# Turning row maxima in 32x32 blocks on VectorE instead of through TensorE and PSUM, and moving them on in 128-byte pieces

## The reference

```
x = x + 0.5 * ffn(layernorm(x))          # ffn: x + msa(ln(x)), then x + moe(ln(x)), top-1 of 8 experts
x = x + attn(layernorm(x))               # 16 query heads, 4 key/value heads, rotary embedding
x = x + 0.5 * ffn(layernorm(x))
scores = q @ k.T / sqrt(8);  attn = softmax(scores, axis=-1);  y = attn @ v
```

## Time and profile before

| | |
|---|---|
| time, median of 3 runs | 1510.23 us (1509.4 to 1512.35) |
| the profiled execution | 1509.52 us; its span 1507.8 us |
| TensorE busy | 1377.5 us (91%) |
| VectorE busy | 1176.0 us (78%) |
| ScalarE busy | 1102.9 us (73%) |
| granted TensorE clock, mean | 0.977 |
| DMA packets | 101485, of them 29792 under 512 B |

### The profile page before, as it was taken

How to read it: one execution, slowest core, us unless ns; L and a number is a source line. 1 busy time by engine, 2 the same in 40 slices (tenths; PEclk the granted TensorE clock), 3 DMA queues, 4 the chain that set the end, 5 groups by cost and what they waited for, 6 DMA issues and landing times.

```text
span 1507.8 us, 34954 instructions
## 1 busy us (share of the span) xinstructions
PE 1377.5 (91%) x12036; PEld 670.6 (44%) x12036; DVE 1176.0 (78%) x1898; ACT 1102.9 (73%) x2124; POOL 646.7 (43%) x983
## 2 busy tenths in 40 slices
PE   3899999999999997999999999999999999999995
PEld 1333333433338883333333333333333344335995
DVE  6888889888855348888888888888888888894541
ACT  2488877787785563888888888787878777777553
POOL 5224245542226683544364353323334543313753
PEclk8799999999999997999999999999999999999998
DMA  3644433433102425432333243333333333211234
GB/s 90 164 137 117 111 102 98 114 93 86 45 25 60 119 75 160 114 83 69 97 97 83 71 110 86 100 91 79 89 93 84 81 88 100 63 37 37 75 106 120
DMA packets 101485, 137.57 MB, mean 91 GB/s; under 512 B 29792, under 2 KB 72160, under 8 KB 101312
## 3 DMA queue, kind: packets, MB, share of 16 engines
q1 hardware_dynamic: 70768, 85.69, 19.9%
q0 software_dynamic: 24256, 45.31, 12.3%
q10 hardware_dynamic: 6288, 4.34, 1.0%
HBM read 79.05 MB, written 53.51 MB: 88 GB/s over the span
## 4 chain that ended last, share of the span: by engine, by line
PE 58%; DVE 28%; issue 7%; DMA 3%; POOL 2%; ACT 1%; SPq 0%; DVEq 0%; POOLq 0%; ACTq 0%
DVE maxima L1251 25%; PE banks L884 16%; PE banks L871 12%; PE banks L855 11%; PE banks L1610 4%; PE banks L912 4%; PE banks L1619 4%; PE banks L894 2%; PE banks L938 2%; PE banks L919 1%; DMA by_token<-work 1%; PE banks L954 1%; DVE split L1259 1%; DVE stats L1329 1%; DMA work<-sorted_x 1%
## 5 line engine op out<-in xcount | busy, mean ns | idle before, releaser
L1251 DVE TENSOR_REDUCE maxima<-banks 128x2 f32<-128x1024 f32 x768 | 924.1, 1222 | 154.9 <-PE banks L855 146.8
L1222 ACT ACTIVATE work<-banks 128x512 f32<-128x512 f32 x1536 | 829.6, 598 | 155.5 <-PE banks L871 140.6
L855 PE MATMUL banks<-K,Q 64*128 64x512 f32 x1536 | 568.2, 459 | 46.5 <-DVE maxima L1251 36.4
L871 PE MATMUL banks<-Q,K 64*128 64x512 f32 x1536 | 566.2, 450 | 0.5
L884 PE MATMUL banks<-work,V 128*18 128x256 f32 x6144 | 481.6, 386 | 1.5 <-ACT work L1222 0.8
L855 PEld LDWEIGHTS banks<-K,Q 64*128 64x128 f32 x1536 | 228.2, 189 | 200.8 <-DVE maxima L1251 135.4
L871 PEld LDWEIGHTS banks<-Q,K 64*128 64x128 f32 x1536 | 228.9, 185 | 177.4 <-ACT work L1222 128.3
L884 PEld LDWEIGHTS banks<-work,V 128*18 128x18 f32 x6144 | 103.3, 96 | 275.1 <-issue 199.8
L723 POOL TENSOR_TENSOR lo<-full,hi 128x512 fp32r<-128x512 f32 x40 | 51.1, 1278 | 245.6 <-ACT hi L1097 144.1
L1619 PE MATMUL banks<-w,work 128*128 x736 | 99.6, 279 | 0.6 <-ACT work L1653 0.6
L1673 DVE COPY work<-w 128x512 f32 x88 | 43.9, 499 | 71.8 <-PE banks L1610 58.6
(11 more groups left out here) (193 smaller groups left out, 1268.4 us busy)
## 6 DMA issues: line engine op xcount, KB each, us to landing
Q<-q_scratch SPq DMA_DIRECT2D x188, 128.0 KB, 2.6
K<-k_scratch SPq DMA_DIRECT2D x376, 64.0 KB, 2.5
Q<-zero_rows SPq DMA_DIRECT2D x182, 64.0 KB, 2.2
q_scratch<-hi POOLq DMA_DIRECT2D x40, 256.0 KB, 4.7
q_scratch<-lo POOLq DMA_DIRECT2D x40, 256.0 KB, 6.8
k_scratch<-hi POOLq DMA_DIRECT2D x20, 256.0 KB, 4.5
k_scratch<-lo POOLq DMA_DIRECT2D x20, 256.0 KB, 6.3
work<-sorted_x SPq DMA_DIRECT2D x76, 66.0 KB, 2.0
```

Source lines behind the costliest of these rows:

```text
L855: fill(nc.tensor.matmul(bank, q4[parts(j), n % SLOTS, j // 2, qt * P:(qt + 1) * P], k4[parts(j), n % SLOTS, j // 2, :], start=True, stop=T ...
L871: nc.tensor.matmul(scp[x % EXPS][:, :], k4[parts(j), n % SLOTS, j // 2, kt * P:(kt + 1) * P], q4[parts(j), n % SLOTS, j // 2, :], start=Tr ...
L1222: nc.scalar.activation(prob[:, kt, j ^ 1, :], scp[x % EXPS][:, :], ACT.Exp, scale=SCALE).then_inc(s.probs, 1)
L1251: nc.vector.tensor_reduce(c.maxima[:, at:at + 9:8], c.banks[:, k * S:(k + 2) * S].rearrange("p (m n) -> p m n", m=2), AX.X, ALU.max).then_ ...
```

## The change

The diff, cut to its core:

```diff
 class Plan:
     def group(self, n, kt):
         names = []
-        if kt == 0 and 1 <= n + 1 < self.last:
-            names += [("rows", n + 1)]
 ...
             def rows_of_max(n):
                 g = n % SLOTS
-                if n:
-                    released(sp, "rows", n)
-                else:
-                    sp.wait_ge(s.first, 2)
+                sp.wait_ge(s.max_turned, n + 1)
                 for tile in range(2):
                     r = TILE * tile + ROWS
-                    sp.dma_start(c.Q[r:r + 2, g * KSLOT:(g + 1) * KSLOT].bitcast(F32).rearrange("i (a n) -> i a n", n=P),
-                                 c.maxT[16 * tile:16 * tile + 16, n % 2 * P:(n % 2 + 1) * P].bitcast(F32))\
-                        .then_inc(s.max_rows[g], 16)
+                    dst = c.Q[r:r + 2, g * KSLOT:(g + 1) * KSLOT].bitcast(F32).rearrange("i (a b q) -> i a b q", b=4, q=32)
+                    for b in range(4):
+                        at = 32 * b + 16 * tile
+                        sp.dma_start(dst[:, :, b, :], c.maxT[at:at + 16, 32 * (n % 2):32 * (n % 2) + 32])                            .then_inc(s.max_rows[g], 16)
 ...
-            def turn_max(n):
-
-                pe.wait_ge(s.split, n + 1)
-                bank = bank_for("rows", n) if n else outp
-                ins = nc.tensor.transpose(bank[0:32, 0:P], c.split[:, 32 * (n % 2):32 * (n % 2) + 32].bitcast(F32), c.ident[:, :])
 ...
                 nc.vector.tensor_tensor(parts[:, :, 1, :], whole, parts[:, :, 0, :].bitcast(F32), ALU.subtract)\
                     .then_inc(s.split, 1)
-
-            def copy_rows(n):
                 if n >= 2:
-                    dve.wait_ge(s.max_rows[(n - 2) % SLOTS], 32 * ((n - 2) // SLOTS + 1))
-                if n:
-                    bank = ring[turns["rows", n].first % RING]
-                    filled(dve, "rows", n)
-                else:
-                    bank = outp
-                    dve.wait_ge(s.first, 1)
-                ins = nc.vector.tensor_copy(cols(c.maxT, n % 2 * P, P), bank[0:32, 0:P])
+                    dve.wait_ge(s.max_rows[(n - 2) % SLOTS], 128 * ((n - 2) // SLOTS + 1))
+                dve.wait_ge(s.split, n + 1)
+                nc.vector.transpose(cols(c.maxT, 32 * (n % 2), 32), cols(c.split, 32 * (n % 2), 32).bitcast(F32))\
+                    .then_inc(s.max_turned, 1)
 ...
-        c.maxT = sb("maxT", [32, 2 * P], F32R)
+        c.maxT = sb("maxT", [P, 2 * 32])
```

More of the change, by code:

```diff
@@ L277 @@
 Turn = namedtuple("Turn", "first end engine done")
-CONSUMER = {"max": "dve", "rows": "dve", "out": "dve", "gate": "dve", "z": "act", "q": "act", "qs": "act", "k": "act",
+CONSUMER = {"max": "dve", "out": "dve", "gate": "dve", "z": "act", "q": "act", "qs": "act", "k": "act",
             "ks": "act", "v": "act", "a": "act", "proj": "act", "n": "act", "rank": "act"}
@@ L396, in stream @@
     if True:
-        s = sems(ctx, nc, f"s{label}", "filled freed evacuated first max_hi split recip max_rows:5 q_loaded:5 k_loaded:5 "
+        s = sems(ctx, nc, f"s{label}", "filled freed evacuated max_hi split max_turned recip max_rows:5 q_loaded:5 k_loaded:5 "
                  "scores probs pv out_copied links dve_links first_stored:2 var_ready std_ready normed renormed stats:2 moments:2 added combined roped hi lo:2 "
@@ L654, in main @@
                 for g in range(SLOTS):
-                    sp.wait_ge(s.max_rows[g], 32 * len(range(g, last, SLOTS)))
+                    sp.wait_ge(s.max_rows[g], 128 * len(range(g, last, SLOTS)))
                 if label == 0:
@@ L856, in max_score @@
                                       k4[parts(j), n % SLOTS, j // 2, :], start=True, stop=True), "max", n, qt, j)
-            def turn_max(n):
-                pe.wait_ge(s.split, n + 1)
-                bank = bank_for("rows", n) if n else outp
-                ins = nc.tensor.transpose(bank[0:32, 0:P], c.split[:, 32 * (n % 2):32 * (n % 2) + 32].bitcast(F32), c.ident[:, :])
-                if n:
-                    fill(ins, "rows", n)
-                else:
-                    ins.then_inc(s.first, 1)
             def score(n, kt, j):
@@ L975, in group @@
                 for kind, i in plan.groups.get((n, kt), ()):
-                    if kind == "rows":
-                        turn_max(i)
-                    elif kind == "rank":
+                    if kind == "rank":
                         rank(i)
@@ L1262, in split_max @@
                     .then_inc(s.split, 1)
-            def copy_rows(n):
                 if n >= 2:
-                    dve.wait_ge(s.max_rows[(n - 2) % SLOTS], 32 * ((n - 2) // SLOTS + 1))
-                if n:
-                    bank = ring[turns["rows", n].first % RING]
-                    filled(dve, "rows", n)
-                else:
-                    bank = outp
-                    dve.wait_ge(s.first, 1)
-                ins = nc.vector.tensor_copy(cols(c.maxT, n % 2 * P, P), bank[0:32, 0:P])
-                if n:
-                    freed(ins, "rows", n)
-                else:
-                    ins.then_inc(s.first, 1)
+                    dve.wait_ge(s.max_rows[(n - 2) % SLOTS], 128 * ((n - 2) // SLOTS + 1))
+                dve.wait_ge(s.split, n + 1)
+                nc.vector.transpose(cols(c.maxT, 32 * (n % 2), 32), cols(c.split, 32 * (n % 2), 32).bitcast(F32))\
+                    .then_inc(s.max_turned, 1)
             def normalise(n):
@@ L1309, in group @@
                 for kind, i in plan.groups.get((n, kt), ()):
-                    if kind == "rows":
-                        copy_rows(i)
-                    elif kind == "out":
+                    if kind == "out":
                         normalise(i)
```

4 lines of the change are left out of this document (1 added, 3 removed).

## The result

The changed kernel takes 1541.8 us (median of 4 runs, 1538.02 to 1544.34) against 1511.29 us (median of 4, 1509.4 to 1513.11): ratio 1.02, 95% interval 1.0172 to 1.0228. It is slower, as forecast, but by 30.5 us where I forecast 10.8, and outside my range. The profiled execution took 1543.42 us with a span of 1541.7, against 1509.52 and 1507.8.

What follows compares the result with a forecast made beforehand. The loop between TensorE and VectorE at group ends was taken as the bound. 14.0 + 3.9 - 8.3 - 0.5 - 1.2 + 2.9 = +10.8 us gave 1521 us, forecast's own range 1512 to 1533, 0.8 range 1501 to 1534.

Steps and rivals of the forecast that it cites:

- Where the loop lies: At group ends: scores, last reduction, split, two reductions, scores; VectorE work put between split and these reductions lengthens the loop.
- The price of the turn: Block turn on VectorE behind the split: delays the next group's first reduction by 0.27 us, ends 0.22 and 0.40.
- y: Time from the block turn's start to the next reduction's start on VectorE: taken as 0.14 us, between 0.09 and 0.27.
- a: Added delay of the reduction behind the block turn: 0.13 us plus the turn's hold on VectorE, 0.27 us in all.
- First kind: 52 group ends where "rows" has "z", "a" or "n" with it: 0.27 us slower each, +14.0 us (11.4 to 20.8).
- Second kind: 26 group ends whose other filling is one long matmul: 0.15 us slower each after 0.12 us spare, +3.9 us.
- Third kind: 14 mid-stream group ends with "rows" alone: a round trip saved, 0.59 us sooner each, -8.3 us (-9.0 to -6.4).
- Starts of the streams: Group 0 of each stream: -1.2 us at the first from sooner reductions, +2.9 us at the second from late maxima.
- my 6.8 us: Landing of the last of eight transfers after the turn: 7 x 0.616 us of issuing plus 2.5 us to landing.
- Mid-stream transfers at nothing: Eight transfers per group within a stream: hidden with 1.5 us to spare in the shortest group, costed at nothing.
- the rows come late: Rival, chance 0.08: at 1.2 us an issue the last transfer is 2.6 us late in shortest groups, about 1560 us.
- -0.5 us that I had for groups 30 and 62: Groups 30 and 62, with no quarter-1 scores left: only TensorE's turn of 0.27 us goes, -0.5 us.

Runs made afterwards that it cites:

- experiment 3: Changed kernel with the block turn moved behind the next group's first two reductions: 1534.62 us, ratio 1.0152 to the kernel before.
- experiment 2: Kernel before, with a block turn added behind the split into a tile that nobody reads: 1530.47 us, ratio 1.0124.
- Experiment 4: Changed kernel with GpSimd's first stores of each stream waiting until group 0's maxima have landed: 1530.4 us, ratio 1.0127 to the kernel before.
- Experiment 1: Kernel before, with TensorE's turn kept but its maxima sent in eight transfers of 128-byte pieces: 1544.83 us, ratio 1.0225.
- 6: Kernel before, with its maxima still sent in two transfers but cut into 128-byte pieces, 128 in all: 1534.18 us, ratio 0.9991.
- 5: Kernel before, with its maxima sent in eight transfers of four 512-byte pieces each: 1551.49 us, ratio 1.0125.

## Why the prediction was right in sign and wrong in size

**Where the loop lies: right.** The block turn stands between the split and the reductions, and each of 78 group ends pays for it. Turned elsewhere (experiment 3), they pay 0.00.

**The price of the turn: nearly right.** I had y = 0.14 us; the reduction starts 1234.37 - 1234.23 = 0.14 us behind L1249. L1249 starts 0.11 us after L1244's end, not the 0.04 that L1261 showed behind L1259 (and that experiment 2's turn shows). So a = 0.33 and net 0.29, against 0.27.

**First kind: right,** 52 x 0.29 = 15.1 us against 14.0.

**Second kind: the step failed that "VectorE has 0.12 us to spare".** I had compared the end of the second reduction with L855. But L855 there follows the long matmul, and that follows the first reduction. An idle gap behind the second reduction is no slack of the first; the whole delay arrives through TensorE. 26 x 0.29 = 7.5 us against 3.9.

**Third kind: the mechanism was right, the size too small.** I took VectorE's 0.59 us and not TensorE's 0.83; 7 of 14 show 0.84, four 0.43 where a stream ends, the sum is -9.9 us against -8.3.

**Starts of the streams: the failing step.** I had -1.2 us for the first and +2.9 for the second; they cost +8.2 and +11.7, which is 18.2 us of the miss of 33.9 - 10.8 = 23.1 (about 2.7 of these 18.2 are the load of keys, below). The step was "Eight issues of 0.616 us put the last at 583.91 + 7 x 0.616 = 588.2, and with 2.5 us from issue to landing, that of the K loads, it is there at 590.7". The first half holds (5.28 us for eight). The second took the landing of a K load in the midst of a stream for a landing at a start, where GpSimd's stores of 256 KB are in the engines; it was 11.6 us at the first start and 7.6 us at the second. The -1.2 us of VectorE are there at the first start (-1.19) but not at the second, where the wait for a load of keys made +1.46 us of them; I had not priced that load, and in experiment 3 (-1.26) it was nearly in time. For the first stream I had priced no transfers at all, though they stand there too. Experiment 4 takes the stores away and finds my 6.8 us as 7.0.

The Trainium skill (DMA: Bandwidth & Descriptors, "Queues, rings and completion order") says that each DMA engine goes around the queues that have work, and drains a whole packet of one before it turns to the next. The traces fit it: GpSimd's queue at 75.0% beside SyncE's at 0.9% while the small pieces are late. They do not show the taking of turns itself, so as a mechanism it stays the page's; what the runs show is the dependence on what GpSimd has queued, on the moment of the issue (3 against the changed kernel, 1 against 6) and on the number of pieces (1 against 5). I had cited the same page for small pieces alone. That part did not bear out: 64 pieces of 128 bytes a transfer cost nothing (0.9991). The Trainium skill (DMA: Bandwidth & Descriptors, "Why small descriptors are slow (HBM only)") says itself that transfers within SBUF do not pay the penalty that it describes.

**Mid-stream transfers at nothing: nearly right for the changed kernel, by luck.** I gave the spare time as 1.5 us against dearer issues. In fact ten waits in the midst of the streams took 8.6 us; eight of them moved no step by more than 0.1 us; the longest is in the +1.9 us of group 49, and one of 0.85 us in group 72. Experiment 1 shows what it really hangs on: with the turn some 2.1 us later, the transfers fall behind the four stores once a batch, +17.5 us in six groups. My rival "the rows come late" was right in kind. Its place (the shortest groups) and its cause (issues of 1.2 us) were wrong, for issues take 5.2 us for eight; and its chance of 0.08 was too low.

**Not considered: the clock.** Behind three of the group ends the granted clock fell to 0.50, 4.5 us in all. Experiment 3, where the group ends have their old length, has nothing in these three groups and half the clock only behind waits for the maxima; experiment 4, with the long ones, has such steps in 9, 61, 73 and 81. So they are more frequent with the block turn in this place. They are not peculiar to it: the second trace of the unchanged kernel has one, +1.48 us in group 37, behind a bare group end where TensorE waited 0.96 and 0.66 us, and experiment 2 has two. Which group end is hit changes from run to run, and no run isolates the idle time as the cause.

**Sum.** 15.1 + 7.5 - 9.9 + 8.2 + 11.7 + 4.5 + 1.9 - 3.9 - 1.6 = +33.5, against 33.9 in the spans. The -0.5 us that I had for groups 30 and 62 lies within the two last terms, which hold the experts too and more than it explains; they are no effect that I can name.

## What to carry to other kernels

Small transfers that something waits for are priced by what stands in the other queues when they are issued: look at the transfers' view of that very stretch, at the starts of stages above all, and prefer two issues ahead of a run of large stores to eight that straddle it. A gap on an engine is slack only for the instruction right before it; follow the delay through the other engine too before crediting it. A change that wins at a few places and loses at many can be kept at the few: here 10 of 96 groups, 0.994.

## What the runs showed of the hardware

- The same eight transfers of 2 KB landed 7.0 us after the first issue without GpSimd's stores beside them, 16.2 us with six of them of 256 KB, while SyncE's next five issues took 10.82 us in place of 2.60.
- Eight such transfers with four stores of 256 KB issued between them made TensorE wait 2.4 to 2.8 us in experiment 1; with two stores between them, it waited for nothing.
- The number of packets under 512 B was no sign of cost here: 42080 in a kernel at 0.9991, 32480 in one at 1.0125.
- A block turn of 128x32 float32 shows as 0.21 us, and VectorE's next instruction starts 0.14 us behind its start, 0.12 us when the turn itself has waited for nothing; the wait of a dependent instruction for its predecessor on VectorE was 0.04 us in one place and 0.11 in another.
